# Waits at the end of SyncE's program: one for every transfer in place of one for each output buffer

## The reference

```python
x = x + _layernorm(_L0_attn_ref(_layernorm(x), W_state, b_state, W_gate, b_gate))
x = x + _layernorm(_L0_ffn_ref(_layernorm(x), ...))

# _L0_attn_ref
px = x @ W_state.T + b_state;  g = sigmoid(x @ W_gate.T + b_gate)
state = tanh(px[t] + state);   out[t] = g[t] * state          # 1024 steps in a row

# _L0_ffn_ref
h = rms(x) * n1;  q, k = rms(heads(h @ wq.T)), rms(heads(h @ wk.T));  v = heads(h @ wv.T)
x = x + (softmax(causal(q k^T / 4)) v) @ wo.T                 # 16 heads of 16; channels 0..63 set to 0
xf = rms(x) * n2;  wts = top2(softmax(xf @ gate.T)), normalised
x = x + sum_e wts[e] * expert_e(xf)                           # 4 experts, hidden 512; channels 0..63 set to 0
```

## Time and profile before

| | us |
|---|---|
| runs | 1611.23, 1610.63, 1606.91 |
| median | 1610.63 |
| the profiled execution | 1611.23 |
| its span, first to last instruction | 1609.5 |

### The profile page before, as it was taken

How to read it: one execution, slowest core, us unless ns; L and a number is a source line. 1 busy time by engine, 2 the same in 40 slices (tenths; PEclk the granted TensorE clock), 3 DMA queues, 4 the chain that set the end, 5 groups by cost and what they waited for, 6 DMA issues and landing times.

```text
span 1609.5 us, 33389 instructions
## 1 busy us (share of the span) xinstructions
PE 1409.7 (88%) x12384; PEld 1116.7 (69%) x12384; DVE 1092.9 (68%) x2898; ACT 987.6 (61%) x2078; POOL 293.7 (18%) x1114
## 2 busy tenths in 40 slices
PE   5914778899998899998989899989989999999997
PEld 2403567789886468788867577767667777777786
DVE  6846576565689777676866795958868669584242
ACT  2435456666556677875565758455656776847941
POOL 2353322322333222222320100000000000000000
PEclk9965578999999899999999999999989999999998
DMA  6582436573666636545756655555656665665543
GB/s 189 155 286 71 124 116 171 168 222 123 187 213 198 184 123 200 186 132 183 216 152 188 188 173 175 166 169 188 194 158 204 181 201 180 189 202 169 156 134 106
DMA packets 195217, 278.50 MB, mean 173 GB/s; under 512 B 33520, under 2 KB 128752, under 8 KB 194800
## 3 DMA queue, kind: packets, MB, share of 16 engines
q1 hardware_dynamic: 195056, 276.37, 56.0%
HBM read 234.18 MB, written 43.45 MB: 172 GB/s over the span
## 4 chain that ended last, share of the span: by engine, by line
PE 54%; DVE 13%; ACT 13%; DMA 6%; issue 5%; POOL 5%; SPq 3%; ACTq 0%; DVEq 0%; POOLq 0%
PE PS L1028 50%; POOL AD L1680 5%; ACT PX L915 4%; ACT work L982 3%; DMA KT<-ktd 3%; DVE mx L1481 2%; PE PS L1031 2%; PE PS L1112 2%; DVE mxb L1481 1%; ACT L982 1%; ACT work L1007 1%; SPq L837 1%; DMA ktd<-KTs 1%; DVE st L1305 1%; ACT KTs L965 1%
## 5 line engine op out<-in xcount | busy, mean ns | idle before, releaser
L915 ACT ACTIVATE PX<-AD 128x8 f32<-128x8 f32 x1023 | 219.6, 215 | 239.4 <-POOL AD L1680 239.3
L982 ACT ACTIVATE work<-PS 128x1024 f32<-128x1024 f32 (+1 forms) x312 | 289.6, 958 | 105.3 <-PE PS L1028 103.7
L1680 POOL TENSOR_TENSOR AD<-PX 128x8 f32<-128x8 f32 x1023 | 245.7, 240 | 582.3 <-ACT PX L915 562.7
L1481 DVE TENSOR_REDUCE mx<-PS 128x2 f32<-128x1024 f32 (+3 forms) x256 | 256.8, 1020 | 84.6 <-PE PS L1028 83.7
L1028 PE MATMUL PS<-work,vlx 128*32 128x256 f32 (+2 forms) x2816 | 240.3, 384 | 21.2 <-ACT work L982 10.8
L1028 PE MATMUL PS<-EP,u_e_l 128*128 128x256 f32 x1024 | 198.4, 288 | 5.5 <-DVE EP L1347 2.3
L1028 PE MATMUL PS<-WB,work 128*128 128x192 f32 x1024 | 187.3, 338 | 11.4 <-DMA WB<-wdn_e_l 6.0
L1028 PEld LDWEIGHTS PS<-WB,work 128*128 128x128 f32 x1024 | 171.2, 196 | 19.5 <-issue 6.8
L1028 PE MATMUL PS<-EP,WB 128*128 128x256 f32 x640 | 182.0, 284 | 0.0
L1028 PE MATMUL PS<-KT,QT 64*128 64x512 f32 (+3 forms) x768 | 150.4, 431 | 33.6 <-DVE mx L1481 11.7
L1028 PEld LDWEIGHTS PS<-EP,u_e_l 128*128 128x128 f32 x1024 | 163.4, 191 | 12.3 <-issue 5.4
(11 more groups left out here) (177 smaller groups left out, 2417.7 us busy)
## 6 DMA issues: line engine op xcount, KB each, us to landing
KT<-ktd SPq DMA_DIRECT2D x112, 512.0 KB, 4.6
WB<-wlo_e_l SPq DMA_DIRECT2D x80, 512.0 KB, 3.9
WB<-wlo_e_up SPq DMA_DIRECT2D x32, 512.0 KB, 4.0
ktd<-KTs SPq DMA_DIRECT2D x128, 128.0 KB, 2.5
WB<-wlo_e_w SPq DMA_DIRECT2D x32, 512.0 KB, 3.6
WB<-wdn_e_down SPq DMA_DIRECT2D x32, 384.0 KB, 3.3
KT<-ktd SPq DMA_DIRECT2D x48, 256.0 KB, 4.0
KT<-ktd SPq DMA_DIRECT2D x32, 384.0 KB, 4.0
```

The source lines that it names most:

```text
L915: eng.activation(cur, AD[n % 2], ACT.Tanh).then_inc(of(*key), 1)
L982: eng.activation(pt[:, :, :, q0:L], two("sc", *a).rearrange("p a (l q) -> p a l q", l=2)[:, :, :, q0:L], ACT.Exp).then_inc(of(*key), 1)
L1481: eng.tensor_reduce(o, two("mxm", *a)[:, :, 0:w], AX, ALU.max, negate=True).then_inc(of(*key), 1)
L1680: eng.tensor_tensor(AD[n % 2], PX[c % 2][:, :, :, t], PX[(n - 1) // L % 2][:, :, :, (n - 1) % L], ALU.add).then_inc(of(*key), 1)
```

## The change

The last loop of SyncE's program is replaced. Before it waited for the last `ost` of each lane; now it goes through all transfers of the plan and calls the helper for each one.

```diff
                 elif kind == "ost":
                     sp.wait_ge(*done("fin", *a))
                     eng.dma_start(rows_in(out, *a), rows_of(*a)).then_inc(of(*key), 16)
-
-            for u in range(NU):
-                if ("ost", u) == max((k for k in plan.order["sp"] if k[0] == "ost" and S.lane(k) == S.lane(("ost", u))),
-                                     key=lambda k: done(*k)[1]):
-                    sp.wait_ge(*done("ost", u))
+            for name, (lane, value) in S.value.items():
+                if name in plan.transfers:
+                    sp.wait_ge(S.sem(lane), value)
```

## The result

| | before | after |
|---|---|---|
| runs, us | 1606.19, 1606.91, 1610.63, 1611.23 | 1619.71, 1625.52, 1628.31, 1630.01 |
| median, us | 1608.77 | 1626.91 |
| the profiled execution, us | 1611.23 | 1626.66 |
| its span, us | 1609.5 | 1624.9 |

The change makes the kernel slower by 1.1%: ratio 1.0106, 95% interval 1.0067 to 1.0146, which is 11 to 23 us. Forecast were +18.4 us. The profiled execution of after is not among the four runs listed.)

What follows compares the result with a forecast made beforehand. The prediction took SyncE's instructions after the last transfer issue to bound the kernel's end: 19.2 us of waits plus 1.0 of crossings less 1.8 is +18.4, so 1610.6 becomes 1629.0 us; range 1626 to 1632, 1622 to 1634 with scatter and rival C.

Steps and rivals of the forecast that it cites:

- SyncE's tail sets the end, one for one: After the last issue at 1606.86, SyncE's work beyond the 1.8 us from 1607.3 to 1609.1 adds fully to the time.
- 296 instructions of two waits: At SyncE's end, 593 waits remain of 683, two per instruction: 296 wait instructions, the branch carrying the 593rd.
- 0.065 us each: Pace of satisfied wait instructions in SyncE's tail, range 0.057 to 0.075 us; 296 of them take 19.2 us.
- The four at 112.5: Four consecutive SyncE wait instructions at 112.5 us, three steps of about 0.067 us, used to bound the pace.
- Three crossings at 0.32: SyncE's tail passes into a next 128-instruction program block three times, 0.32 us extra each, 1.0 us together.
- The 1.7 us of standing still vanish: SyncE's wait for the last transfer's landing, some 1.7 us before, comes in the 296th instruction, after the landing.
- Sum: SyncE's tail: 19.2 + 1.0 = 20.2 us, less the former 1.8, gives +18.4 us and 1629.0 us.
- Rival A: Satisfied waits in SyncE's tail cost only their recorded 28 or 17 ns: +7.5 or +4.2 us; chance 0.08.
- Rival B: SyncE's tail keeps one wait per lane, 21 instructions, 1.4 us inside the landing wait; time stays 1610.6; chance 0.04.
- Rival C: In SyncE's tail, fetch lags (2 us a crossing) or each semaphore costs extra: +5 us, 1634; chance 0.08.

Runs made afterwards that it cites:

- the one of 184 instructions: The changed kernel's loop without the 224 weight-piece waits; ratios to the kernel before 1.0021 (1614.30 against 1610.95 us) and, in a later set, 1.0078 (1621.21 against 1608.63).
- the run with 20 instructions: The changed kernel's loop cut to one wait for each of the 41 lanes; 1607.88 against 1610.95 us for the kernel before, ratio 0.9995.
- 638 instructions: The changed kernel with all 683 waits again behind its own, none skipped; 1645.10 against 1610.95 us for the kernel before, ratio 1.0217.

## Why the prediction was right

Its steps, one by one:

- **SyncE's tail sets the end, one for one.** Shown in the profile, where the tail grew by 17.2 us and VectorE stood at the block's end for it; the median grew by 18.1. The times of the other tails agree within their intervals or, for the one of 184 instructions, in one set of two. But all four means lie under the tail's growth: 4.7 us for 5.8, 8.0 for 10.1, 14.4 for 17.2 and 35.0 for 38.6. Whether that is scatter stays open. Waits of the same kind placed on GpSimd or ahead of the last issue cost nothing, or the 2.6 us that stuck out.
- **296 instructions of two waits.** The profile counts them, and from 65 L566 goes to 359 on SyncE as foretold.
- **0.065 us each.** 0.061 in the row of 128. The term was over by 296 x 0.004 = 1.2 us. The gaps beside transfers had given 0.06 to 0.08: the step from a transfer to a wait is a little longer than that from a wait to a wait. The four at 112.5 were the better row, but it is read to 0.1 us only. The mechanism was right and this size a little off.
- **Three crossings at 0.32.** Three at 0.3, in the places that counting on by 128 gives.
- **The 1.7 us of standing still vanish.** Yes: the wait for the last transfer is in the last instruction, and L566 has no wait in the tail that the profile shows. That it did so hung on where the compiler put it, as the run with 20 instructions shows, where it did not vanish whole.
- **Sum.** +18.4 forecast, +17.2 by the tail, +18.1 by the medians; 1629.0 forecast, 1626.9 measured. The median of before also came out 1.9 us lower with one more run. That 18.1 comes within 0.3 us of 18.4 is luck, since the interval is 11 to 23 us; the 1.2 us by which the tail missed is the error of the sum.

Rival A, cheap waits, falls with the pace of 0.061: the record of 28 ns is less than half of what an instruction takes. Rival B, one wait per lane, did not happen in the change, but the run with one wait for each lane shows that its forecast was right, no difference in the times; the tail was 0.7 us longer where it had none. Rival C falls with 638 instructions at the same pace and no step above 0.4 us; its 2 us for a crossing came from no row, and no run shows it. The Trainium skill ("Runtime: NRT & Kernel Launch", section Instruction fetch mechanics) has an issue floor of about 20 cycles an instruction, an estimated 17 ns at the clock that the prediction cites. The trace does not agree that this is the price of a wait: 61 ns were measured for this form.

One thing in the prediction was too sure: that a measurement of this kernel tells 0.3% from no change. With 19 to 24 runs of before, which spread over 15 to 19 us in a set, the intervals of single comparisons were 0.2 to 0.4% to either side, and one of them missed its 0.62% by more than its half-width. It did not matter for 1.1%.

## What to carry to other kernels

A wait whose semaphore is long high is not free: it is an instruction (0.061 us for two waits on SyncE here), and at the end of a program, where the last transfer has been issued and all engines wait for one, such instructions add up undivided, as the 17.2 us of the change did. Semaphores that count up need one wait for their last value, not one for each. Of those that remain, the slowest belongs last: by the rows of the run with 20 instructions this would have saved its 0.7 us, but no run tried it. Others can stand ahead of the last issue or on an engine that is done, as two runs showed. To find such a tail, compare the end of the chain of work with the end of the span: 2.7 us lay between them before, and 19.9 after.

## What was not expected of the hardware

- Of the price of a satisfied wait instruction on SyncE (0.061 us in a row) the record shows 28 ns; on GpSimd it is 0.086 us with 43 ns in the record. Times added up from records are short by half, and a wait that stood 1.7 us for a landing has a record of 28 ns as well: read starts, not lengths.
- SyncE passes from one 128 of its instructions to the next with 0.3 us extra, the same at 8 us a block as in the body, where 128 instructions took over 200 us, and five times in a row.
- The body of this program, unchanged, ended anywhere from 1595.3 to 1613.0 us in profiled executions (last issues at 1595.3 in the second run of the change and 1597.8 with the waits on GpSimd; in the run with the waits ahead of the issue VectorE was done at 1613.0). What makes it vary by that much was not tested, but the record has something that goes with it, TensorE's granted clock (its mean over the span, near the upper of its two levels, 2.4 GHz). Over the 63 runs of the kernel before in the three sets, time and clock have a correlation of -0.69; the fastest, 1596.28 us, had 0.946 of full speed and the slowest, 1617.93 us, 0.930.
